# First stage of a gated transformer stack: the shift of x moves to ScalarE, the rounding constant goes in PSUM copies, PE's side jobs and the last product are placed anew

## What is computed

```python
def _smooth_quant_linear(x, w):
    amax_x, amax_w = max|x| and max|w| over rows, per column
    s  = sqrt(amax_x / amax_w)
    xs, ws = x / s, w * s
    x_scale, w_scale = max|xs|, max|ws| per row, over 127
    x_q, w_q = round(xs / x_scale), round(ws / w_scale)   # clipped to +-127
    return x_q @ w_q.T * x_scale * w_scale.T

def _expert_forward(xe, guw, dw):       # one batch
    gate, up = split(_smooth_quant_linear(xe, guw))       # 512 -> 2 x 256
    return _smooth_quant_linear(silu(gate) * up, dw)      # 256 -> 512

x = x + tanh(g_xattn[0]) * _expert_forward(layernorm(x), fside, ctx)
```

## Time and profile before

| | us |
|---|---|
| median of three runs | 1400.13 |
| lowest, highest run | 1398.43, 1401.13 |
| the profiled execution's own time | 1398.27 |
| its span in the trace | 1396.6 |
| mean granted clock of PE | 0.93 of full |

### The profile page before, as it was taken

The page is one execution under the profiler, slowest core; times in us unless marked ns, Lnnn a source line. Parts: engine busy times, 40 slices in busy tenths (PEclk is TensorE's granted clock), DMA queues, the critical chain, the costliest instruction groups (busy, mean ns, idle before and its releaser), DMA issues. The chain is left out here.

```text
span 1396.6 us, 16561 instructions
## 1 busy us (share of the span) xinstructions
PE 1165.5 (83%) x5256; PEld 504.7 (36%) x5317; DVE 860.0 (62%) x1325; ACT 654.6 (47%) x1147; POOL 413.2 (30%) x479
## 2 busy tenths in 40 slices
PE   5775875999799999963459988998999999876897
PEld 3443432555444444431013222222322222223453
DVE  7899875214245555315798887778777777226543
ACT  2554452555322222241347666556655556724543
POOL 3475470010132222113334432222222220015332
PEclk8987898999989999985669999999999999996999
DMA  7223123444244444337813332322222220017011
GB/s 262 88 103 121 53 98 135 153 138 150 87 159 146 150 143 149 115 110 228 188 50 104 89 107 68 89 80 86 71 85 85 74 74 2 3 10 84 35 38 46
DMA packets 106356, 141.58 MB, mean 101 GB/s; under 512 B 20788, under 2 KB 75572, under 8 KB 106280
## 3 DMA queue, kind: packets, MB, share of 16 engines
q1 hardware_dynamic: 87432, 111.37, 25.0%
q0 software_dynamic: 18368, 28.85, 8.0%
q10 hardware_dynamic: 480, 0.39, 0.1%
HBM read 97.44 MB, written 46.27 MB: 103 GB/s over the span
## 5 line engine op out<-in xcount | busy, mean ns | idle before, releaser
L2394 DVE TENSOR_REDUCE a_top<-PS 128x2 f32<-128x1024 f32 x256 | 308.4, 1222 | 94.8 <-PE PS L2155 90.8
L2241 ACT ACTIVATE a_E<-PS 128x512 f32<-128x512 f32 x512 | 277.7, 596 | 150.0 <-PE PS L2138 149.8
L2138 PE MATMUL PS<-a_Q,a_K 99*128 99x512 bf16 (+1 forms) x469 | 157.0, 386 | 16.6 <-ACT a_E L2241 6.2
L2155 PE MATMUL PS<-a_K,a_Q 64*128 64x512 bf16 x512 | 104.2, 405 | 48.9 <-DVE a_top L2394 29.6
L1367 PE MATMUL PS<-f_W,f_GT 128*128 x312 | 141.6, 597 | 0.0
L2168 PE MATMUL PS<-a_E,a_V 128*32 128x512 f32 x1024 | 136.9, 607 | 0.4 <-ACT a_E L2241 0.4
L2138 PEld LDWEIGHTS PS<-a_Q,a_K 99*128 99x128 bf16 (+1 forms) x512 | 44.2, 97 | 155.4 <-ACT a_E L2241 105.4
L1771 POOL TENSOR_TENSOR a_qf<-a_qf,a_tab 128x512 f32<-128x512 f32 x15 | 19.1, 1270 | 269.3 <-DVE a_swapped L2338 269.3
L1423 DVE TENSOR_TENSOR f_H<-f_SG,PS 128x256 f32<-128x256 f32 x39 | 16.4, 421 | 125.2 <-ACT f_SG L1407 125.2
L1367 PEld LDWEIGHTS PS<-f_W,f_GT 128*128 128x128 f32 x312 | 56.9, 192 | 57.2 <-issue 57.2
L2155 PEld LDWEIGHTS PS<-a_K,a_Q 64*128 64x128 bf16 x512 | 24.7, 93 | 141.9 <-issue 72.4
(11 more groups left out here) (361 smaller groups left out, 2006.2 us busy)
## 6 DMA issues: line engine op xcount, KB each, us to landing
f0r_raw<-in_L_ffn_W_dram SPq DMA_DIRECT2D x24, 512.0 KB, 4.6
a_K<-k_parts SPq DMA_DIRECT2D x192, 64.0 KB, 2.3
a_Q<-a_q_parts SPq DMA_DIRECT2D x186, 64.0 KB, 2.4
f_y<-f_Y SPq DMA_DIRECT2D x39, 256.0 KB, 2.0
v_units<-V SPq DMA_DIRECT2D x16, 512.0 KB, 2.8
a_V<-v_units SPq DMA_DIRECT2D x16, 512.0 KB, 3.8
k_parts<-f_k_parts SPq DMA_DIRECT2D x16, 384.0 KB, 3.4
a_q_parts<-a_parts SPq DMA_DIRECT2D x16, 384.0 KB, 2.8
```

The lines of the kernel that those rows point to most:

```text
L2138: nc.tensor.matmul(PS[:, 4 + h % 2, :], K6[k][0:rows_, o, head // 2, kt * P:(kt + 1) * P], Q6[k][0:rows_, o, head // 2, :], start=True, st ...
L2155: last = nc.tensor.matmul(PS[:, 2 * pair + o, :], Q6[k][at, o, h // 2, t * P:(t + 1) * P], K6[k][at, o, h // 2, :], start=True, stop=True)
L2241: nc.scalar.activation(E[step % 2][:, h, :], PS[:, 4 + h % 2, :], ACT.Exp).then_inc(exp_done, 1)
L2394: nc.vector.tensor_reduce(top[:, h - h % 2:h - h % 2 + 2, t], PS[:, 2 * pair:2 * pair + 2, :], AX.X, ALU.max).then_inc(maxed, 1)
```

## The change

Four things are changed in the first stage.

1. **Rounding.** ACT adds ROUNDER to x as well (`shift_x`, 4 activations with scale). The bf16 tiles xq and wq are gone: PE turns the shifted f32 tiles, and ROUNDER is taken off in the copies out of PSUM: on ACT for upper weights (two copies of 1024 columns) and both lower operands, on DVE for upper x (`take_up_x`, two instructions of 1024 columns).
2. **Order and banks.** PE turns the upper weight half of banks 2 and 3 first, the lower weights next, the half of banks 0 and 1 last. The fourth lower product goes to bank 0, in the last step to bank 5.
3. **Side jobs.** Seven slots; 10, 7, 7, 7 and 9 jobs in the five steps. In steps 0 and 4 they alternate between bank 7 and a second bank, and PE may be one job ahead of ACT.
4. **Layernorm.** Its small tiles hold all batches; the statistics of batch 2 are taken at the end of step 0, those of batch 3 in step 1, none later. In step 0 `normalize(1)` comes behind `take_up`.

Banks and PE's helpers:

```diff
-        DOWN_AT = (4, 5, 6, 4)
+        DOWN_AT = (4, 5, 6, 0)
+        LAST_AT = (0, 1, 2, 5)
...
+            def turn_shifted(q, half, banks, done):
+                for c in range(2 * half, 2 * half + 2):
                     for t in range(4):
+                        last = nc.tensor.transpose(PS[:, banks[c % 2], t * P:(t + 1) * P], q[:, t, c * P:(c + 1) * P], identf[:])
                 last.then_inc(done, 1)
...
+            def finish_up(u):
+                pe.wait_ge(up.w_shifted, u + 1)
+                turn_shifted(up.ws, 0, (2, 3), up.wqT_done)
+                pe.wait_ge(up.wsc_row_ready, u + 1)
+                pe.wait_ge(up.x_scaled, u + 1)
+                turn_shifted(up.ws, 1, (0, 1), up.wqT_done)
+                pe.wait_ge(up.x_shifted, u + 1)
+                for half, banks in ((0, (2, 3)), (1, (0, 1))):
+                    pe.wait_ge(up.wqT_ready, 2 * u + half + 1)
+                    turn_shifted(up.xs, half, banks, up.xqT_done)
+
+            def finish_down(d):
+                pe.wait_ge(down.w_shifted, d + 1)
+                pe.wait_ge(down.wsc_row_ready, d + 1)
+                turn_shifted(down.ws, 0, (4, 5), down.wqT_done)
+                pe.wait_ge(down.x_shifted, d + 1)
+                pe.wait_ge(down.wqT_ready, d + 1)
+                turn_shifted(down.xs, 0, (4, 6), down.xqT_done)
```

PE's queue as it is after the change, the steps and then the last one (removed lines left out, kept ones marked as new too):

```diff
+            for i in range(NB):
+                u, d = i, i - 1
+                pe.wait_ge(up.w_loaded, 16 * (u + 1))
+                if u:
+                    pe.wait_ge(hs_ready, u * TB)
+                turn_w(up, u, 1, 2)
+                if d >= 0:
+                    pe.wait_ge(down.w_loaded, 16 * (d + 1))
+                    if d:
+                        pe.wait_ge(y_ready, d * TB - 2)
+                    turn_w(down, d, 0, 4)
+                    if d:
+                        pe.wait_ge(y_ready, d * TB)
+                turn_w(up, u, 0, 0)
+                if u == 0:
+                    side.tensor_start(pe)
+                side.tensor(pe, i, 0)
+                pe.wait_ge(up.x_ready, u + 1)
+                pe.wait_ge(up.reduced, 4 * u + 1)
+                turn_x(up, u, 1, 2)
+                pe.wait_ge(up.reduced, 4 * u + 2)
+                turn_x(up, u, 0, 0)
+                if d >= 0:
+                    turn_down_x(d)
+                s_rows(up, u, (0, 0), (1, 0))
+                side.tensor(pe, i, 1)
+                if d >= 0:
+                    s_rows(down, d, (6, 0), (6, 256))
+                side.tensor(pe, i, 2)
+                wsc_row(up, u, 1)
+                side.tensor(pe, i, 3)
+                side.tensor(pe, i, 4)
+                if d >= 0:
+                    wsc_row(down, d, 4)
+                finish_up(u)
+                side.tensor(pe, i, 5)
+                if d >= 0:
+                    finish_down(d)
+                pe.wait_ge(up.xqT_ready, 2 * u + 2)
+                for t in range(TB):
+                    product(up, t, t)
+                if d >= 0:
+                    pe.wait_ge(down.xqT_ready, d + 1)
+                    for t in range(TB - 1):
+                        product(down, t, DOWN_AT[t])
+                side.tensor(pe, i, 6)
+                if d >= 0:
+                    pe.wait_ge(hs_ready, u * TB + 1)
+                    product(down, TB - 1, DOWN_AT[TB - 1])
+            d = NB - 1
+            pe.wait_ge(down.w_loaded, 16 * NB)
+            pe.wait_ge(y_ready, d * TB - 2)
+            turn_w(down, d, 0, 4)
+            pe.wait_ge(hs_ready, NB * TB)
+            side.tensor(pe, NB, 0)
+            turn_down_x(d)
+            side.tensor(pe, NB, 1)
+            s_rows(down, d, (6, 0), (6, 256))
+            side.tensor(pe, NB, 2)
+            wsc_row(down, d, 4)
+            side.tensor(pe, NB, 3)
+            pe.wait_ge(down.w_shifted, NB)
+            pe.wait_ge(down.wsc_row_ready, NB)
+            turn_shifted(down.ws, 0, (4, 5), down.wqT_done)
+            side.tensor(pe, NB, 4)
+            pe.wait_ge(down.x_shifted, NB)
+            pe.wait_ge(down.wqT_ready, NB)
+            turn_shifted(down.xs, 0, (4, 6), down.xqT_done)
+            side.tensor(pe, NB, 5)
+            pe.wait_ge(y_ready, d * TB)
+            pe.wait_ge(down.xqT_ready, NB)
+            for t in range(TB):
+                product(down, t, LAST_AT[t])
+            side.tensor(pe, NB, 6)
```

ACT's new helpers:

```diff
+            def shift_x(L, b):
+                act.wait_ge(L.x_scaled, b + 1)
+                for t in range(4):
+                    last = nc.scalar.activation(L.xs[:, t, :], L.xs[:, t, :], ACT.Copy, bias=ROUNDER,
+                                                scale=L.inv_scale[:, t:t + 1])
+                last.then_inc(L.x_shifted, 1)
+
+            def take_up_w(u):
+                for half, bank in ((0, 2), (1, 0)):
+                    act.wait_ge(up.wqT_done, 2 * u + half + 1)
+                    nc.scalar.activation(up.wqT[:, 2 * half:2 * half + 2, :], PS[:, bank:bank + 2, :], ACT.Copy,
+                                         bias=-ROUNDER).then_inc(up.wqT_ready, 1)
+
+            def take_down_w(d):
+                act.wait_ge(down.wqT_done, d + 1)
+                nc.scalar.activation(down.wqT[:], PS[:, 4:6, :], ACT.Copy, bias=-ROUNDER).then_inc(down.wqT_ready, 1)
+
+            def take_down_x(d):
+                act.wait_ge(down.xqT_done, d + 1)
+                nc.scalar.activation(down.xqT[:], PS[:, 4:7:2, :], ACT.Copy, bias=-ROUNDER).then_inc(down.xqT_ready, 1)
```

ACT's queue as it is after the change, in the same manner:

```diff
+            for i in range(NB):
+                u, d = i, i - 1
+                if d >= 0:
+                    side.scalar(act, d, 6)
+                    side.scalar_waves(act, d)
+                    silu(d)
+                side.scalar(act, i, 0)
+                root(up, u)
+                if d >= 0:
+                    root(down, d)
+                    if u < NB - 1:
+                        norm_root(u + 1)
+                side.scalar(act, i, 1)
+                side.scalar(act, i, 2)
+                shift_w(up, u)
+                take_wsc_row(up, u, 1)
+                side.scalar(act, i, 3)
+                shift_x(up, u)
+                if u == 0:
+                    norm_root(1)
+                side.scalar(act, i, 4)
+                take_up_w(u)
+                if d >= 0:
+                    shift_w(down, d)
+                    take_wsc_row(down, d, 4)
+                    shift_x(down, d)
+                side.scalar(act, i, 5)
+                if d >= 0:
+                    take_down_w(d)
+                    take_down_x(d)
+                if u == 0:
+                    act.wait_ge(gates_loaded, 32)
+                    nc.scalar.activation(tg[:], gates[:], ACT.Tanh).then_inc(tg_ready, 1)
+            d = NB - 1
+            side.scalar(act, d, 6)
+            silu(d)
+            side.scalar(act, NB, 0)
+            side.scalar_waves(act, d)
+            side.scalar(act, NB, 1)
+            root(down, d)
+            side.scalar(act, NB, 2)
+            shift_w(down, d)
+            take_wsc_row(down, d, 4)
+            side.scalar(act, NB, 3)
+            shift_x(down, d)
+            take_down_w(d)
+            side.scalar(act, NB, 4)
+            take_down_x(d)
+            side.scalar(act, NB, 5)
+            side.scalar(act, NB, 6)
```

DVE: the quantization and the order of the end of a step:

```diff
-            def quantize_w(L, b):
-                v.wait_ge(L.w_shifted, b + 1)
-                nc.vector.tensor_scalar(L.wq[:], L.ws[:], ROUNDER, None, ALU.subtract).then_inc(L.wq_ready, 1)
-
-            def quantize_x(L, b):
-                ch.wait()
-                for t in range(4):
-                    ch.step(nc.vector.tensor_scalar(L.xs[:, t, :], L.xs[:, t, :], L.inv_scale[:, t:t + 1], ROUNDER, ALU.mult, ALU.add))
-                ch.wait()
-                nc.vector.tensor_scalar(L.xq[:], L.xs[:], ROUNDER, None, ALU.subtract).then_inc(L.xq_ready, 1)
+                nc.vector.reciprocal(L.inv_scale[:, 0:4], L.scale[:, 0:4]).then_inc(L.x_scaled, 1)
+
+            def take_up_x(b):
+                for half, bank in ((0, 2), (1, 0)):
+                    v.wait_ge(up.xqT_done, 2 * b + half + 1)
+                    nc.vector.tensor_scalar(up.xqT[:, 2 * half:2 * half + 2, :], PS[:, bank:bank + 2, :], ROUNDER, None,
+                                            ALU.subtract).then_inc(up.xqT_ready, 1)
...
+                    row_stats(1)
+                if u == 1:
+                    row_stats(3)
+                take_up_x(u)
+                if u:
+                    if u < NB - 1:
+                        normalize(u + 1)
+                    take_up(u)
+                else:
+                    take_up(u)
+                    normalize(1)
+                    row_stats(2)
+                if d >= 0:
+                    take_down(d, False)
```

Side jobs:

```diff
-    IN_SLOT = (1, 0, 3, 2, 2)
+    SECOND = {0: 6, 4: 3}
+    FILL = ((1, 0, 3, 1, 1, 2, 2),) + ((1, 0, 2, 1, 1, 1, 1),) * 3 + ((1, 1, 1, 1, 1, 1, 3),)
...
+            bank = self.bank_of(i, (b, kind, n))
```

(45 more changed lines are left out.)

164 lines of the change are left out of this document (45 added, 119 removed).

## The result

The changed kernel takes 1393.45 us (median of 5 runs, 1390.61 to 1394.75), the kernel before on the same chip 1401.13 (1398.43 to 1403.46): ratio 0.994, 95% interval 0.9923 to 0.9957. It is faster by 0.6%, in a range forecast as 1380 to 1397, with 1388.4 as the likeliest. The profiled execution took 1391.41, its span 1389.6.

The account below looks back on a forecast made before the run. DVE sets the pace of steps 1 to 3 before, a chain through ACT and PE after. +2.9 - 5.5 - 6.5 - 2.4 - 1.9 = -13.4, less 1.7 for the clock, -11.7: median 1388.4 us, range 1380 to 1397.

Parts of the forecast that it names:

- the walk: First stage, its chain added up item by item at the high clock: -13.4 us over all steps.
- clock allowance: Whole stage: 1.7 us allowed for side jobs or turns at PE's low clock, making the net -11.7.
- DVE's relief: Step 1: 9.9 us leave DVE, two PSUM subtractions add 2.4 (1.22 each, 0.60 from below), net -7.5.
- What costs nothing: Hidden work: SP's stores, POOL's angle chain (27.31 us of POOL in step 1), extra f32 turns outside the chain.
- The chain through ACT as the new bound: Step 1: ACT and PE alternate, products start at 34.8 us, step lasts 43.4 against 48.9, DVE idles.
- DVE keeps the pace: Rival: ACT's chain is shorter than walked, steps of 41.5 us, about -24, kernel 1376; chance 0.08.
- Its signs: Steps 1 to 3: DVE idle some 5 us, first reductions 43 to 45 apart; step 1 begins at 54 to 56.
- Step 0: Ten PE jobs instead of eight before step 1: products start at 45.5, first reduction at 55.3, +2.9 us.
- Step 2: V jobs where step 1 turned context, 1.3 more ahead of `shift_w`: 44.6 us against 51.1, -6.5.
- step 3: From its first reduction to its products: 36.0 us against 38.4, -2.4.
- Last step: Step 3's products to the next stage: 42.0 us against 43.9, -1.9, including some 2 for the root's table load.
- slower: Rival: PE stays at the low clock through each step's finish, 6.5 us per step, +9, kernel 1409; chance 0.07.

Follow-up runs that it names:

- rounding_before: Changed kernel with the rounding back on DVE (bf16 tiles turned, plain ACT copies), new slots and order kept: 1404.46 us, 1.0028 of the kernel before.
- old_slots: Changed kernel with eight side jobs in each step as before and one bank only: 1417.87 us, 1.013 of the kernel before.
- shift_on_vector: Changed kernel with ROUNDER added to upper and lower x by DVE instead of ACT: 1392.05 us, 0.9939 of the kernel before.
- filler: Changed kernel with twelve idle turns of the identity ahead of the rows of s in steps 0 to 3: 1383.55 us, 0.988 of the kernel before.
- root_first: Changed kernel with ACT's lower root ahead of slot 1's K job in the last step: 1390.11 us, 0.9921 of the kernel before.
- the run again: The changed kernel measured once more, unedited: 1387.72 us, 0.991 of the kernel before.
- lower_shift: Changed kernel with only the lower x shift moved from ACT back to DVE: 1387.68 us, 0.9904 of the kernel before.
- stats_late: Changed kernel with the statistics of batches 2 and 3 taken one step later: 1391.89 us, 0.9941 of the kernel before.
- three: Changed kernel with idle turns in all five steps, lower x shift on DVE and last step's root first: 1384.37 us, 0.9892 of the kernel before.
- four: Changed kernel with idle turns in all five steps, lower x shift on DVE, last root first and later statistics: 1383.30 us, 0.9883 of the kernel before.

## Why the prediction was right, and where it was off

The forecast's median was 1388.4. The first measurement gave 1393.45, a gain of 7.7 for 11.7, the second 1387.72, a gain of 13.1. The stage's own 8.6, which repeated, is the firmer number: 13.4 was the walk, 11.7 with the clock allowance.

- **DVE's relief**: right in its prices. 0.60 to 1.22 was the open one, 1.20 it was. The net fell short: from first reduction to first reduction of step 1 DVE was busy 45.98 before and 40.0 after, 6.0 less for a forecast 7.5. The missing 1.4 is `normalize`: 3.6 (L510) instead of 2.2 (L438). It now runs beside POOL's angle chain, and took 1.92 in step 0 with POOL idle; that this is the cause is not tested, but the forecast had put the chain under "What costs nothing". With DVE's work back (rounding_before) nothing is left of the gain. With the old counts of jobs (old_slots) neither, which the forecast did not see: it gave one job less behind the products 1.8 us a step (10.4 to 8.6), and the run showed over 6.
- **The chain through ACT as the new bound**: right in steps 2 and 3, where DVE waits 3.3 and 2.4 us for PE's turns of `xs_up` and 5.2 us of work put back on it (shift_on_vector) cost nothing. In step 1 only half right. The products did start behind the chain, 34.6 for 34.8, but DVE was busy 94% of the step, as before the change, and 4.5 of the 5.2 us put back on it came through. DVE and the chain end together there, and a step within 0.8 us of the walk, near the rival's 41.5 too, doesn't tell them apart. *DVE keeps the pace* was wrong for the stage by steps 0, 2 and 3.
- **Its signs**: the four activations, the copies and the subtractions came as said, and the upper products were at the high level. But steps 1 to 3 were 42.6, 45.9 and 43.7 long for "43 to 45", the idle stretches "of some 5 us" were none, 3.3 and 2.4, step 1 began at 57.4 for "54 to 56", and one V copy of the last step was released by a DMA, a sign of being wrong that cost 1.3.
- **Step 0**, "the products start at 45.5 ... +2.9": the term failed by 2.1 us. They started at 48.2. The larger error is the clock: I walked with the high level and allowed 1.7 us for the whole stage, where in step 0 alone the granted clock was 0.53 (the low level is 0.50) from 22 to 35 us, and 1.00 after, to 48. The angles and the first two K jobs took 4.9 us more than at the high level (3.78 and 6.73 for 2.06 and 3.60), and 1.3 came ahead of the first ratio. That is more than the 2.7 us by which the products were late, so the walk itself was 3 us or more too long and hid part of it; the filler run says the same (45.51 with 3.1 us of low level left in it).
- **Step 2** (-5.2 for -6.5) and **step 3** (-1.6 for -2.4): in step 2 the angles took 3.8 and a V job 3.7 us, together 3.5 more than at the high level. The step is 1.3 longer than forecast; that these two jobs made it so is argued, not tested alone.
- **Last step**, "two us are the root's table load": I had it behind sines and a copy, but not behind a job at the low level. It cost 3.1 with the copy, and root_first gives them back: -0.3 for -1.9.
- **The clock allowance**: 1.7 in the sum; idle turns give back 6.4 in the changed kernel and 3.7 in the kernel before, and in neither all of it, since low stretches were left. This is the term that made 8.6 out of 13.4. The *slower* rival had a mechanism that occurs, in the wrong place: the low level lay behind PE's wait for the root, not over the finish. In rounding_before it did lie over the upper products.
- The rest of the kernel was 1.5 us longer in this profile and 1.4 shorter in the run again (1160.5) than before (1161.9), and up to 1166.0 elsewhere; changes of a median by 4 us can be this alone.

The bank of the fourth lower product, the second bank of steps 0 and 4 and the turned order of the upper weights were not tried by themselves. What also stays open is why small reorderings moved the low level between steps by 1 to 3 us each (lower_shift, root_first, stats_late), and the first ratio by up to 2.2; and whether three edits beat the idle turns alone, which the medians of five runs do not settle. Filler, at 0.988 of before, beats the kernel before; the changed kernel of the same group had 0.991, with intervals that touch (0.9862 to 0.9898 and 0.9889 to 0.993). Neither three nor four is shown to beat filler.

## What to carry to other kernels

When work leaves the bounding engine for a chain across two others, walk that chain with durations at both clock levels: here the gain forecast at the high level was 13.4 us and 8.6 came. Look for the wait of PE that stands ahead of its longest jobs, and fill it with something harmless. Parts of a change that look separate may be worth something only together: try each alone before keeping or dropping one. And before a gain of a us or two is put down to an edit, look whether it stands behind the first instruction that the edit can reach: 1.3 of lower_shift's 1.5 us did not.

## What the runs showed of the hardware

- Twelve f32 turns of the identity, 1.5 us of PE, cut a wait of 2.70 us to 1.28 and kept the granted clock up over most of the work behind it: angles 2.06 instead of 3.78 us, step 0 at 0.92 instead of 0.84. The Trainium skill (TensorE: Matmul & The Clock Gate, "Part 4: PE-mode transpose") says that the high clock does not engage for transposes. The traces differ: sixteen f32 turns took 1.91 to 1.94 at a granted 1.00 and 3.51 at 0.53, and the idle turns kept the level up.
- An f32 shift with scale on ACT, 512 columns, cost 0.64 each in a row of four (2.56), less than DVE's 3.4 for the same four. And 1024 f32 columns out of PSUM took ACT 0.97 to 1.03, less than DVE's 1.20.
- The profile of one kernel repeated within 0.1 us inside the stage, while the ratios of the same kernel against the kernel before were 0.994 and 0.991 in two measurements (their intervals overlap).
